# A half tile's 64 rows stacked twice on the partitions in the last step of three Down products

## The reference

```python
x = x + jnp.tanh(g_xattn[0]) * _L0_xattn_ref(_layernorm(x, axis=-1), ctx_4096, ctx_4096, Wq, Wk, Wv, Wo)
x = x + jnp.tanh(g_ffn[0]) * _L0_ffn_ref(_layernorm(x, axis=-1), W_gate, W_up, W_down)
# _L0_ffn_ref, on 16 x 128 = 2048 tokens of 1024, F = 2752
up = xt @ W_up.T
gate = jax.nn.silu(xt @ W_gate.T)
y = gate * up @ W_down.T
```

## Time and profile before

| | |
|---|---|
| median of 3 runs (lowest to highest) | 1894.93 us (1894.23 to 1895.89) |
| the profiled execution, time of the run | 1895.36 us |
| its span from the first to the last instruction | 1893.5 us |
| mean granted TensorE clock | 0.999 of full |
| busy share of the span: PE, DVE, ACT, POOL | 99%, 66%, 44%, 46% |

### The profile page before, as it was taken

How to read it: one execution, slowest core, us unless ns; L and a number is a source line. 1 busy time by engine, 2 the same in 40 slices (tenths; PEclk the granted TensorE clock), 3 DMA queues, 4 the chain that set the end, 5 groups by cost and what they waited for, 6 DMA issues and landing times.

```text
span 1893.5 us, 27278 instructions
## 1 busy us (share of the span) xinstructions
PE 1882.8 (99%) x9298; PEld 1552.1 (82%) x9298; DVE 1243.1 (66%) x1716; ACT 834.3 (44%) x1963; POOL 867.6 (46%) x632
## 2 busy tenths in 40 slices
PE   9999999999999999999999999999999999999999
PEld 7888888888887788888888788888888888888887
DVE  7878887787787855555554677775555555546565
ACT  5863783683584533333332354543333333333433
POOL 1430440251255598888888220225656666630000
PEclk9999999999999999999999999999999999999999
DMA  6235316326324244454445876752323232267665
GB/s 212 90 127 176 104 60 251 99 63 228 118 75 184 101 161 160 161 174 170 151 170 199 297 253 214 246 193 73 120 89 111 87 121 96 89 216 251 212 229 181
DMA packets 127195, 298.76 MB, mean 158 GB/s; under 512 B 12672, under 2 KB 24448, under 8 KB 121728
## 3 DMA queue, kind: packets, MB, share of 16 engines
q1 hardware_dynamic: 126960, 297.45, 46.0%
q10 hardware_dynamic: 144, 0.13, 0.0%
HBM read 221.25 MB, written 71.57 MB: 155 GB/s over the span
## 4 chain that ended last, share of the span: by engine, by line
PE 95%; DMA 2%; POOL 2%; DVE 1%; issue 0%; ACT 0%; SPq 0%; POOLq 0%; DVEq 0%; ACTq 0%
PE ps L1623 28%; PE ps L1625 28%; PE ps L1624 28%; PE ps L1673 3%; PE ps L1664 2%; PE ps L1684 2%; PE ps L1665 2%; PE ps L1835 1%; PE ps L1721 1%; DMA raw<-ws 1%; DMA ws<-dw 1%; PE ps L1844 0%; DMA kv_raw<-in_wc 0%; DMA dw<-in_wd 0%; POOL wsum L825 0%
## 5 line engine op out<-in xcount | busy, mean ns | idle before, releaser
L1623 PE MATMUL ps<-xop_h,w_h 128*128 128x512 f32 x1208 | 472.2, 391 | 0.0
L1625 PE MATMUL ps<-xop_h,w_l 128*128 128x512 f32 x1208 | 470.6, 390 | 0.0
L1624 PE MATMUL ps<-xop_l,w_h 128*128 128x512 f32 x1208 | 470.5, 389 | 0.0
L1191 DVE TENSOR_TENSOR bl<-raw,bh 128x1024 fp32r<-128x1024 f32 x154 | 199.6, 1305 | 128.0 <-ACT bh L883 127.8
L1625 PEld LDWEIGHTS ps<-xop_h,w_l 128*128 128x128 f32 x1208 | 227.0, 188 | 47.4
L1624 PEld LDWEIGHTS ps<-xop_l,w_h 128*128 128x128 f32 x1208 | 227.0, 188 | 46.4
L1623 PEld LDWEIGHTS ps<-xop_h,w_h 128*128 128x128 f32 x1208 | 226.9, 188 | 46.4 <-DVE cc L1435 0.3
L883 ACT ACTIVATE bh<-raw 128x1024 fp32r<-128x1024 f32 x154 | 163.2, 1062 | 219.3 <-PE ps L1625 187.6
L1191 DVE TENSOR_TENSOR w_l<-fraw,w_h 128x512 fp32r<-128x512 f32 x130 | 136.0, 1047 | 186.0 <-ACT w_h L883 186.0
L1623 PE MATMUL ps<-bh 128*128 128x512 f32 x616 | 241.7, 392 | 1.1 <-DVE bl L1191 1.0
L730 POOL TENSOR_TENSOR pb<-pb,rinv 128x512 f32<-128x512 f32 x128 | 154.9, 1211 | 186.6 <-DVE rinv L1247 186.6
(11 more groups left out here) (161 smaller groups left out, 3416.3 us busy)
## 6 DMA issues: line engine op xcount, KB each, us to landing
fraw<-in_wf SPq DMA_DIRECT2D x42, 1024.0 KB, 5.2
raw<-hs SPq DMA_DIRECT2D x154, 256.0 KB, 3.1
hs<-hsum SPq DMA_DIRECT2D x22, 1280.0 KB, 5.7
raw<-ws SPq DMA_DIRECT2D x110, 256.0 KB, 4.1
wc_raw<-in_wc SPq DMA_DIRECT2D x44, 512.0 KB, 4.5
dw<-in_wd SPq DMA_DIRECT2D x11, 1024.0 KB, 7.8
hs<-hb SPq DMA_DIRECT2D x44, 256.0 KB, 2.0
raw<-in_wd SPq DMA_DIRECT2D x44, 256.0 KB, 3.6
```

The source lines that it names most:

```text
L1191: return nc.vector.tensor_tensor(out, whole, hi.bitcast(F32), ALU.subtract)
L1623: pe.matmul(out, w_hi_, m_h, start=first, stop=False, skip_group_check=goes_on)
L1624: pe.matmul(out, w_hi_, m_l, start=False, stop=False, skip_group_check=goes_on)
L1625: return pe.matmul(out, w_lo_, m_h, start=False, stop=last, skip_group_check=goes_on)
```

## The change

In the last step of products m = 4, 5 and 6 the 64 rows that count are loaded twice, to partitions 0 to 63 and to 64 to 127, for h and for the weights. After the rounding, DVE puts the low part of h in place of the high part on partitions 64 to 127. One matmul with the high weights (which stand in both halves) then adds high x high and low x high together, and a second with the low weights adds high x low (and low x low besides). So each of the four pieces takes 2 matmuls in place of 3.

```diff
+HALF_ROWS = tuple(m for m, (hx, wx, _) in enumerate(DOWN) if hx in (3, H_A22) or wx in (4, W_B22))
...
+        def half_rows(n):
+            return n // PAIRS_B in HALF_ROWS and n % PAIRS_B == PAIRS_B - 1
...
+                if half_rows(n):
+                    for e, part in enumerate((hs[s][q][hx], wd[2 * q + 1, :, HALF:D] if wx == W_B22 else ws[q][wx])):
+                        (step_n, _), (step_1, _) = part.ap
+                        rows = bass.AP(part.tensor, part.offset, [[0, 2], [step_n, FR], [step_1, HALF]])
+                        sp.dma_start(raw[k][:, e, :], rows).then_inc(raw_in[k], 16)
+                    return
...
+                if half_rows(n):
+                    minus(bl[n % RING][:, 1, :], raw[n % RAWS][:, 1, :], bh[n % RING][:, 1, :])
+                    below = bh[n % RING][FR:P, 0, :]
+                    minus(below, raw[n % RAWS][FR:P, 0, :], below).then_inc(b_lo, 1)
+                    return
...
-                    ins = three(ps[:, banks[g % len(banks)], :], hi[:, 0, toks], lo[:, 0, toks], hi[:, 1, :], lo[:, 1, :],
-                                f == 0, f == PAIRS_B - 1)
+                    place = ps[:, banks[g % len(banks)], :]
+                    if half_rows(n):
+                        pe.matmul(place, hi[:, 0, toks], hi[:, 1, :], start=False, stop=False)
+                        ins = pe.matmul(place, hi[:, 0, toks], lo[:, 1, :], start=False, stop=True)
+                    else:
+                        ins = three(place, hi[:, 0, toks], lo[:, 0, toks], hi[:, 1, :], lo[:, 1, :], f == 0, f == PAIRS_B - 1)
```

## The result

The changed kernel takes 1925.41 us (median of 5 runs, 1923.95 to 1926.05), the kernel before 1894.57 us beside it (1894.23 to 1895.89): a ratio of 1.0159, 95% interval 1.0148 to 1.017, so 30.8 us slower, with 24 matmuls less to do. The forecast was 1922.0 us, with a range of 1898 to 1938.

The account below looks back on a forecast made before the run. PE was taken as the bound (95% of the span), DVE close behind. Load waits 24.2 + clock and what follows 8 - removed matmuls 5.44 + about 0.6 gave +27 us: 1922.0 us, range 1898 to 1938.

Parts of the forecast that it names:

- The pitch as price: PE in Down: a matmul costs its start distance, 0.2267 us, so 24 removed save at most 5.44 us.
- DVE's waits taken off: Ends of products 4 to 6: with loads on time, DVE's adds and subtractions hold PE; 3.1 us remain saved.
- The loads: Six last-step loads: two engines carry 112 more rows each at 85 ns, so they land 9.5 us later.
- The assumption that the first count sets the number of engines: Last-step loads: a transfer is cut along its first dimension, so a leading 2 puts it on two engines.
- The waits: PE ahead of steps 54, 65, 76 in both passes: six waits of 2.8 to 4.9 us, 24.2 us together.
- The clock and what follows: Behind the six waits: lower granted clock and late subtractions, 1.5 us for five and 0.5 for the last, 8 us.
- the 1.7 per wait: Trace before: PE idles 1.86 us, then runs at the 1.2 GHz level for 3.5 us, losing 1.7 us.
- DVE as the next bound: Ends of Down products: DVE has only 0.7 us to spare, so PE arriving earlier waits, 0.15 us at step 56.
- the rival's mechanism: Last-step loads on time, engines sharing them as before, DVE decides: 3.1 us saved, 1891.8 us; chance 0.11.

Follow-up runs that it names:

- row loads: Changed kernel, each half of the six last-step loads written as two transfers of 64 rows, to partitions 0-63 and 64-127; 1891.8 us, ratio 0.9986.
- Two-first: Kernel before, 12 matmuls per step and no row read twice; only the six loads of steps 54, 65, 76 read as 2 x 64 rows; 1928.73 us, ratio 1.0185.
- the clock kept: Changed kernel, with 34, 22 and 42 small PE transposes ahead of the waits for steps 54, 65 and 76 in pass 0; 1923.4 us, ratio 1.0157.
- four first: Kernel before, only the six loads of steps 54, 65, 76 read as 4 x 32 rows; 1895.18 us, ratio 1.0003.

## Why the prediction was right

**The pitch as price.** 24 matmuls at 0.2267 us were to be 5.44 us. Where nothing waits this is seen directly: in the run with row loads step 54 of pass 1 starts at 1826.60 and step 55 at 1828.41, 1.81 us for eight matmuls in place of 2.72 for twelve. As a whole the row loads saved 2.7 us, and 3.1 were forecast with DVE's waits taken off. Two-first is 3.3 us above the changed kernel, but that pair differs in its waits and clock stretches too.

```profile
1826.60 0.39 PE L1956 MATMUL ps<-bh 128*128 128x512 f32 x1
...
1828.41 0.39 PE L1642 MATMUL ps<-bh 128*128 128x512 f32 x1
```

**The loads.** 9.5 us later by 112 rows of 85 ns: 9.15 measured on average, on two engines by the share of 0.13. The assumption that the first count sets the number of engines rested on no row of the kernel before; it was argued from the pattern and weighed with the Trainium skill's rule. By that rule ("DMA: Bandwidth & Descriptors", "Why a DMA increments its semaphore by 16 and not by 1") 2, 4 and, for 64 rows, 16 engines are used; the traces agree: 6, 10 and 64 semaphore steps, and 0.13 of the engines busy for 2.

**The waits.** 24.2 us forecast, 22.0 measured; nearly all of the difference is the 0.35 us by which each of the six loads was less late (3.4, 2.4, 4.2, 3.7, 4.4, 3.8 against 2.9, 2.8, 4.9, 4.8, 4.2, 4.6).

**The clock and what follows.** 8 us forecast for both. By the windows the clock took 13.5 us, more than the 1.7 per wait, since three of the stretches were much longer than the one in the earlier trace rows. Late subtractions cost little beside it: from 1190 us on PE's weight loads waited 1.1 us for DVE beside the six steps' own waits. This is the term that was sized too small, and the waits were sized 2.2 us too large, so the two errors partly cancel in the 1922.0.

The account by the spans: 22.0 + 13.5 - 1.7 - 5.4 = 28.4 of the 30.1 us between 1923.6 and 1893.5. The 1.7 are the stretch of the earlier trace rows, which the profiled run of the kernel before had lost and the changed kernel's had not. The other 1.7 are not laid to a place here, though the 0.11 us that a restarted matmul takes longer and the adds at the end belong to it.

**DVE as the next bound.** It was the rival's mechanism, and with the loads on time it came out as worked out: 1891.8 us forecast, 1891.8 measured (closer than its runs agree, which spread over 2.4 us), the wait for step 56 of pass 1 0.14 us against 0.15.

## What to carry to other kernels

A transfer's price is in its pattern as well as in its bytes: look at which count stands first, and when a broadcast wants a 2 there, write two transfers that each have the rows first. Before matmuls are taken away from a busy PE, price them by the distance of their starts, and look how far behind each wait's releaser already is; here 5.44 us of matmuls taken away brought 2.7 us. A wait of PE can cost again by the clock behind it: here those of 2.4 to 4.4 us all did, and by more than one earlier stretch in the trace had led to expect.

## What the runs showed of the hardware that was not expected

The half-speed stretch behind a wait was about 3.5 us long in some of the windows above and 6 to 7 us in others. The one in the window from 1277.90 began before its wait was over: PE was busy for 5.31 us of seven. In the run with the clock kept, a wait of 0.3 us where 2.4 us had been left no such stretch.

Shorter waits did not always lower the clock. The idleness of the earlier trace rows (1.8 to 1.9 us) is in all nine profiled runs, and the half-speed stretch behind it only in two of them, the kernel before and four first: the mean clock from 630 to 640 us is 0.83 in these and 1.00 in the other seven. In two first PE idled 1.47 us ahead of step 54 of pass 0 and the clock stayed at 1.00 for the six microseconds behind. So the one stretch from which the prediction took its 1.7 us was itself not certain to come.

While the two engines worked through their 128 rows each, SP took longer to issue as well: the next step's h load, usually issued in 0.33 us and behind 1170 us of the kernel before never in more than 1.87, took 2.71 us behind step 54 and 3.24 behind step 65 of pass 1.

```profile
1830.54 2.71 SPq L582 DMA_DIRECT2D raw<-hs  x1
...
1866.35 3.24 SPq L582 DMA_DIRECT2D raw<-hs  x1
```
